# Five score banks in attention, and the LoRA gate chain moved from GpSimd to VectorE

## What is computed

```python
x = L0_attn_resid_pre                       # (16, 2048, 2048) f32
x = x + attn(layernorm(x), Wq, Wk, Wv, Wo)  # 16 heads of 128, causal, ALiBi
x = x + ffn(layernorm(x), W, b, lora_A, lora_B, gate_w, gate_b)

# attn
scores = jnp.clip(q @ k.T / sqrt(128), -1024.0, 1024.0) + alibi_and_causal_mask
z = softmax(scores) @ v                      # then the output projection Wo
# ffn: a linear layer plus a top-2 mixture of 8 LoRA experts of rank 16
base = x_flat @ W.T + b
topk_logits, topk_idx = top_k(x_flat @ gate_w.T + gate_b, 2)
gates = softmax(topk_logits)
out = base + sum_over_2_experts(gates * (x_flat @ A_e.T @ B_e.T))
```

## Time and profile before

| what | us |
|---|---|
| median of the 2 runs shown | 4903.23 |
| lowest and highest of them | 4753.82, 5052.64 |
| the profiled execution | 4754.08 |
| its span, slowest core (core 6) | 4752.5 |
| PE busy | 3613.1 (76%) |
| DVE busy | 1807.8 (38%) |
| ACT busy | 1149.5 (24%) |
| POOL busy | 248.3 (5%) |
| granted TensorE clock, mean of core 6 | 0.809 |

### The profile page before, as it was taken

How to read it: one execution, slowest core, us unless ns; L and a number is a source line. 1 busy time by engine, 2 the same in 40 slices (tenths; PEclk the granted TensorE clock), 3 DMA queues, 4 the chain that set the end, 5 groups by cost and what they waited for, 6 DMA issues and landing times. The chain is left out here.

```text
span 4752.5 us, 65283 instructions; the slowest of 8 cores (4735.4 to 4752.5 us)
## 1 busy us (share of the span) xinstructions
PE 3613.1 (76%) x18150; PEld 1718.8 (36%) x18452; DVE 1807.8 (38%) x4848; ACT 1149.5 (24%) x2606; POOL 248.3 (5%) x786
## 2 busy tenths in 40 slices
PE   2587878888887794777735878888888877947777
PEld 1233434434433341333312334344344333423333
DVE  3435455455464110222234354554554641112222
ACT  3323233232242100111133232332332421001111
POOL 0000000000000001111100000000000000011111
PEclk8687888878878896888856878888788778968888
DMA  4211110110101646111131111101101016461111
GB/s 114 58 23 19 19 23 14 23 19 14 26 16 34 156 157 115 63 63 71 54 121 57 23 19 19 23 14 23 19 14 26 16 33 164 149 121 66 63 63 62
DMA packets 55537, 258.38 MB, mean 54 GB/s; under 512 B 13720, under 2 KB 13984, under 8 KB 34720
## 3 DMA queue, kind: packets, MB, share of 16 engines
q0 software_dynamic: 36464, 119.66, 12.6%
q1 hardware_dynamic: 11824, 84.20, 5.5%
q10 hardware_dynamic: 6912, 50.33, 3.0%
HBM read 273.15 MB, written 67.11 MB: 72 GB/s over the span
## 5 line engine op out<-in xcount | busy, mean ns | idle before, releaser
L852 ACT ACTIVATE prT<-dg,cstt 128x128 bf16<-128x128 f32 (+1 forms) x576 | 216.4, 386 | 1806.9 <-DVE dg L824 1176.9
L813 DVE TENSOR_SCALAR sp<-ps 128x512 f32<-128x512 f32 (+3 forms) x1104 | 631.3, 593 | 13.6 <-ACT prT L877 4.0
L806 PE MATMUL ps<-QT,KT 128*128 128x512 bf16 (+3 forms) x1044 | 465.3, 483 | 206.2 <-DVE sp L813 158.0
L1118 PE MATMUL cb<-wf,cT 128*128 128x512 bf16 x1984 | 523.6, 425 | 97.3 <-DMA wf<-wf 81.0
L877 ACT ACTIVATE prT<-sp,cstt 128x128 bf16<-128x128 f32 (+2 forms) x1368 | 578.8, 488 | 16.6 <-DVE sp L813 9.7
L420 PE MATMUL bp<-wo,zTt 128*128 128x512 bf16 x2006 | 467.9, 394 | 99.3 <-DMA wo<-wo 75.4
L633 PE MATMUL pp<-xnT,wv 128*128 128x512 bf16 x1980 | 459.8, 391 | 6.3 <-DVE zc L753 2.0
L633 PE MATMUL pp<-xnT,wq 128*128 128x512 bf16 x2014 | 454.7, 384 | 2.2 <-issue 0.4
L633 PE MATMUL pp<-xnT,wk 128*128 128x512 bf16 x2014 | 450.4, 381 | 2.1 <-issue 0.4
L744 PE MATMUL pz<-va,prT 128*128 128x129 bf16 x3652 | 390.1, 264 | 27.9 <-ACT prT L877 12.1
L1118 PEld LDWEIGHTS cb<-wf,cT 128*128 128x128 bf16 x2048 | 217.1, 108 | 393.4 <-issue 216.0
(11 more groups left out here) (105 smaller groups left out, 2404.2 us busy)
## 6 DMA issues: line engine op xcount, KB each, us to landing
bx<-x SPq DMA_DIRECT2D x32, 1024.0 KB, 6.8
x2d<-b POOLq DMA_DIRECT2D x32, 1024.0 KB, 8.8
c<-x2d ACTq DMA_DIRECT2D x32, 1024.0 KB, 4.8
out<-co SPq DMA_DIRECT2D x32, 1024.0 KB, 3.9
prT<-x ACTq DMA_DIRECT2D x16, 1024.0 KB, 5.6
prT<-x SPq DMA_DIRECT2D x16, 1024.0 KB, 5.8
wv<-wv POOLq DMA_DIRECT2D x32, 512.0 KB, 6.0
wq<-wq POOLq DMA_DIRECT2D x32, 512.0 KB, 6.0
```

The source lines that it names most:

```text
L806: lambda e, c=c, q0=q0, n=n, bank=bank: e.matmul(psc[bank][:, 0:n], KT[:, c * 128:(c + 1) * 128], QT[:, q0 * 128: q0 * 128 + n], start=Tru ...
L813: lambda e, n=n, bank=bank, buf=buf: e.tensor_scalar(spanb[buf][:, 0:n], psc[bank][:, 0:n], 1024.0, -1024.0, ALU.min, ALU.max),
L852: soff=soff: e.activation(probsT[:, pslot:pslot + min(ncols, 128)], diagb[:, soff:soff + min(ncols, 128)] if ncols == 64 else diagb[:, 0:128],
L1118: lambda e, bi=bi, dc=dc, og=og, bk=bk: e.matmul(b["pb"][bk][:, :], b["xnT2"][bi][:, dc * 128:(dc + 1) * 128], b["wfT"][:, dc * D + og * 5 ...
```

## The change

Two edits.

The first gives the score matmuls five PSUM banks. The two projection banks, idle while a head's scores are made, join the three score banks in one list, and the spans go round over five. Two guards are carried over at the head's start and two at its end, so that no bank is written before it has been read. The three SBUF buffers `spanb` between DVE and ACT stay three.

The second puts all 18 POOL operations of the gate chain on DVE. Their arithmetic, operands and order stay; the waits on `s_pool` become waits on `s_dve`.

```diff
@@ _plan_head
+    banks = [psc[0], psc[1], psc[2], ppb[0], ppb[1]]
+    st["sc_guard"][3] = max(st["sc_guard"][3], st["proj_evac"][0])
+    st["sc_guard"][4] = max(st["sc_guard"][4], st["proj_evac"][1])
...
-            bank = si % 3
+            bank = si % 5
             buf = si % 3
...
-                           psc[bank][:, 0:n],
+                           banks[bank][:, 0:n],
...
-                           spanb[buf][:, 0:n], psc[bank][:, 0:n],
+                           spanb[buf][:, 0:n], banks[bank][:, 0:n],
...
     st["probsT_guard"] = s_pe.n
+    st["proj_evac"][0] = max(st["proj_evac"][0], st["sc_guard"][3])
+    st["proj_evac"][1] = max(st["proj_evac"][1], st["sc_guard"][4])
@@ _plan_ffn
-                        inc=s_dve, waits=[(s_pe, glmm), (s_pool, gl_user)])
+                        inc=s_dve, waits=[(s_pe, glmm), (s_dve, gl_user)])
...
-        t = pg.op("gpsimd",
+        t = pg.op("vector",
                   lambda e: e.tensor_scalar(g[:, 8:16], b["gl"][:, :],
                                             g[:, 0:1], None, ALU.is_equal),
-                  inc=s_pool, waits=[(s_dve, t)])
+                  inc=s_dve, waits=[(s_dve, t)])
...
-                    inc=s_pe, waits=[(s_pool, wv_tok), (s_dve, wts_evac)])
+                    inc=s_pe, waits=[(s_dve, wv_tok), (s_dve, wts_evac)])
```

More of the change, by code:

```diff
@@ L278, in _build_seq @@
                       span_exp=[0, 0, 0], pz_guard=[0, 0],
-                      sc_guard=[0, 0, 0], vaug_ones=s_pool.n, vaug_reader=0,
+                      sc_guard=[0, 0, 0, 0, 0], vaug_ones=s_pool.n,
+                      vaug_reader=0,
                       vts_tok=0, arep_tok=0, arep_user=0,
@@ L1016, in _plan_ffn @@
                   inc=s_dve, waits=[(s_dve, gl_evac)])
-        t = pg.op("gpsimd",
+        t = pg.op("vector",
                   lambda e: e.tensor_scalar(g[:, 8:16], b["gl"][:, :],
                                             g[:, 0:1], None, ALU.is_equal),
-                  inc=s_pool, waits=[(s_dve, t)])
-        t = pg.op("gpsimd",
+                  inc=s_dve, waits=[(s_dve, t)])
+        t = pg.op("vector",
                   lambda e: e.tensor_tensor(g[:, 40:48], g[:, 8:16], IOTA,
                                             ALU.mult),
-                  inc=s_pool, waits=[(s_pool, t)])
-        t = pg.op("gpsimd",
+                  inc=s_dve, waits=[(s_dve, t)])
+        t = pg.op("vector",
                   lambda e: e.tensor_scalar(g[:, 48:56], g[:, 8:16],
                                             -1e9, 1e9, ALU.mult, ALU.add),
-                  inc=s_pool, waits=[(s_pool, t)])
-        t = pg.op("gpsimd",
+                  inc=s_dve, waits=[(s_dve, t)])
+        t = pg.op("vector",
                   lambda e: e.tensor_tensor(g[:, 24:32], g[:, 40:48],
                                             g[:, 48:56], ALU.add),
-                  inc=s_pool, waits=[(s_pool, t)])
+                  inc=s_dve, waits=[(s_dve, t)])
         t = pg.op("vector",
@@ L1068, in _plan_ffn @@
                                             AX.X, ALU.min),
-                  inc=s_dve, waits=[(s_pool, t)])
-        t = pg.op("gpsimd",
+                  inc=s_dve, waits=[(s_dve, t)])
+        t = pg.op("vector",
                   lambda e: e.tensor_scalar(g[:, 16:24], IOTA,
                                             g[:, 33:34], None, ALU.is_equal),
-                  inc=s_pool, waits=[(s_dve, t)])
-        t = pg.op("gpsimd",
+                  inc=s_dve, waits=[(s_dve, t)])
+        t = pg.op("vector",
@@ L1075, in _plan_ffn @@
                   lambda e: e.tensor_tensor(g[:, 34:35], g[:, 1:2],
                                             g[:, 0:1], ALU.subtract),
-                  inc=s_pool, waits=[(s_pool, t)])
+                  inc=s_dve, waits=[(s_dve, t)])
         te = pg.op("scalar",
                    lambda e: e.activation(g[:, 35:36], g[:, 34:35], AF.Exp),
-                   inc=s_act, waits=[(s_pool, t)])
-        t = pg.op("gpsimd",
+                   inc=s_act, waits=[(s_dve, t)])
+        t = pg.op("vector",
@@ L1082, in _plan_ffn @@
                   lambda e: e.tensor_scalar(g[:, 36:37], g[:, 35:36],
                                             1.0, None, ALU.add),
-                  inc=s_pool, waits=[(s_act, te)])
+                  inc=s_dve, waits=[(s_act, te)])
         t = pg.op("vector",
                   lambda e: e.reciprocal(g[:, 37:38], g[:, 36:37]),
-                  inc=s_dve, waits=[(s_pool, t)])
-        t = pg.op("gpsimd",
+                  inc=s_dve, waits=[(s_dve, t)])
+        t = pg.op("vector",
                   lambda e: e.tensor_tensor(g[:, 38:39], g[:, 35:36],
@@ L1097, in _plan_ffn @@
+        t = pg.op("vector",
                   lambda e: e.tensor_scalar(g[:, 48:56], g[:, 16:24],
                                             g[:, 38:39], None, ALU.mult),
-                  inc=s_pool, waits=[(s_pool, t)])
-        wv_tok = pg.op("gpsimd",
+                  inc=s_dve, waits=[(s_dve, t)])
+        wv_tok = pg.op("vector",
                        lambda e: e.tensor_tensor(g[:, 16:24], g[:, 40:48],
                                                  g[:, 48:56], ALU.add),
-                       inc=s_pool, waits=[(s_pool, t)])
+                       inc=s_dve, waits=[(s_dve, t)])
```

30 lines of the change are left out of this document (15 added, 15 removed).

## The result

| | before | changed |
|---|---|---|
| profiled execution, us | 4754.08 | 4715.89 |
| its span, slowest core | 4752.5 | 4714.4 |
| lowest of all executions | 4749.48 (26 runs) | 4711.48 (27 runs) |
| median of all executions | 4857.80 | 4798.47 |
| ratio of undisturbed executions | | 0.9926, 95% interval 0.9900 to 0.9952 |

A forecast was written before the change was run, and what follows sets the result against it. It took DVE's list to bound a head's rows and, in stage C, the gate chain on POOL to end slightly later than PE's first half. 4754.1 - 33 (gate chain) + 0 (banks) = 4721 us, range 4680 to 4780.

The forecast's parts named there:

- The bound in attention: Rows of a head: bound by DVE's list, PE's 158 us wait for score banks is slack; five banks bring 0.
- The seam (third rival): Between a head and the next projection: 30 seams lose 1.78 us each to the clock, +53, 4774 us; chance 0.08.
- The price of the chain: Gate chain on DVE in stage C: 6.7 us after MAX8's 0.16, against 8.39 for all of it before.
- The wait at twt: PE's wait for POOL before the twt transpose in stage C: goes whole, -24.2 us.
- My split of it: Of the 24.2 us waited at twt, 18 lie in the 24 periods and 6 in the other eight tiles.
- The clock in stage C: Without the wait at twt, second halves of 7.07 us come in two tiles of three, from about one in four.
- Two to one gives 30.86, so 1.12 us a tile: Stage C: two tiles at 30.60 us to one at 31.37, against 31.98 before; 26.9 us in 24 periods.
- an edge: Clock around twt in stage C: nearly equal first halves (8.55 and 8.49 us), second halves 1.7 us apart.
- The sum: Whole kernel: 4754.1 - 33 for the gate chain + 0 for the banks = 4721 us; chance 0.60.
- The range: Whole kernel's time: 4680 to 4780 us, with 4700 to 4740 for the forecast itself.
- nothing in this trace explains that. My number is for an execution like the profiled one: Whole kernel: median 4903 us lies half way between the two runs shown; the forecast follows the lower, profiled one.
- The rule against the banks: Score matmuls in attention: cycling through more PSUM banks could make the clock go back and forth; only the seam could lose.

The follow-up runs named there:

- The runs without clips: Changed kernel without the clip on spans that don't hold the diagonal block: ratio to the kernel before 0.9816 with three banks, 0.9476 with five.
- The padded chain: Changed kernel with seven more small unused DVE operations in the gate chain, which takes 8.43 us: ratio to the kernel before 1.0023.
- The added 0.27 us: Changed kernel with one small DVE operation between the copy of the gate weights and the matmul that spreads them: ratio to the kernel before 0.9926.
- the added 0.81 us: Changed kernel with three chained small DVE operations between the copy of the gate weights and the matmul that spreads them: ratio to the kernel before 0.9996.

## Why the prediction was right, and where it was wrong

**The bound in attention: right.** I read DVE as the bound from 3.2 us of waiting in 1104 clips and priced the banks at 0, with ends of -3 and +53. Alone they gave a ratio whose interval holds 1, a head's period didn't move, and 89 of 99 us of wait turned up at the transpose of z, as the text had said. The runs without clips show that this depends on DVE: the same edit is then worth 3.4%.

**The seam (third rival): not seen.** The V projections in the middle heads take 13.76 us, before and after.

**The price of the chain: right within 0.3 us.** I had 6.7 us after MAX8; it took 6.37. The plain steps on eight columns take 0.166 to 0.172 us, 0.01 more than I assumed, with gaps of 0.10 where I had 0.115; those with a column as scalar 0.231, not 0.214, but their follower starts 0.11 us later and not 0.16. The wait at twt went from 24.2 to 0.7 us; I had all of it. My split of it was off: the 24 periods held 16.1 us and not 18, so the other eight tiles had 8.1. The padded chain shows that its end is what counts.

**The clock in stage C: right in sign and size, and partly for another reason.** The step "Two to one gives 30.86, so 1.12 us a tile" measured 30.69 and 1.29. I expected the short second half in two tiles of three; it was 19 of 32. The tiles that stay without it cost less than the 31.37 us I gave them, because they come with a first half of 7.1 us, not 7.63: the period to the tile before is then about 29 us, and the pair averages under 31. I had also thought that every wait near twt pulls towards the slow clock. The added 0.27 us was absorbed in most tiles; the added 0.81 us cost double. What I had called an edge is there, but it has a side on which a wait is nearly free.

**The sum: -33 against -38.** The 24 periods gave -30.8 us (I had -26.9). From the first to the last twt of the two stages the time fell by 21.2 and 20.0 us, so the remaining tiles gave about 10 where I had 6; outside these stretches some 3 us came back, spread over stages that the change doesn't touch.

**The range: wrong as stated.** The step that failed is "nothing in this trace explains that. My number is for an execution like the profiled one": the sum put the distance from a profiled execution to the median of all at nothing. It measured 83 us after (4798.5 - 4715.9) and 104 us before (4857.8 - 4754.1), more than twice the effect of the change, and so the median lies 18 us above my upper end of 4780. The two runs that I had, 6% apart, said that the median of a new set could lie anywhere between them. A range for that number has to hold this, and mine held only the terms of the change. Why it is there stays open: the lower clock of the row under the result goes with it, and no run here says what lowers the clock. Measured on the profiled execution, 4715.9, or as a ratio, 0.9930 within 0.9900 to 0.9952, the forecast holds.

**The rule against the banks.** More banks did no harm here. The score matmuls went round over five banks in attention, and the projections behind the heads run at full clock as before. Without the clips the granted clock in a head's rows rose from 0.73 with three banks to 0.89 with five. The Trainium skill, "TensorE: Matmul & The Clock Gate", section "A second HAM failure mode: psum-queue depth-cycling", tells of a clock that goes back and forth in a kernel that cycles through banks, and blames the engine's short idle times between groups of matmuls. The runs without clips agree on the idle times and not on the cycling: with more banks PE had fewer waits and a higher clock.

## What to carry to other kernels

A wait between two engines is worth its length only if the one waited for is ever idle for the other; look at both directions before giving it buffers. If the answer is no, the edit isn't useless but early: take load off the bound engine, and it may pay, as it did here with 3.4% (where the banks were also held longer).

A chain of tiny dependent operations is hidden or not by where it ends. Compare its end with the end of the work beside it in the shortest such stretch, and count again after every change that shortens that stretch. And read what stands in front of a late operation on its own engine's list: the largest gain of this study in a kernel that computes everything, 3.0%, came from moving a layer norm ahead of additions that weren't ready.

## What was not expected of the hardware

- On [128, 8] operands a step of a dependent chain takes 0.27 us on DVE (0.34 with a column as scalar), and the whole chain with its 18 steps on POOL took 8.39 us against 6.53. MAX8 and the reduce are as fast on DVE as an elementwise step (0.16 us).
- The length of a tile in stage C isn't a smooth function of its waits. Waits of about 0, 0.27 and 0.81 us more gave periods of 30.69, 30.90 and 32.43 us. Second halves at 7.07 us (clock 1.00) became more with the first, 23 of 32 against 19, and vanished with the second. Why the clock falls on one side or the other isn't shown.
- Taking a wait of 4.4 us out of a tile gave 5.0 us; putting the chain back on POOL then cost 1.74 us a tile, where it had cost 1.29.
